# Moving half of a key gather from GpSimd to VectorE in a bilevel routing attention kernel

## What is computed

```python
xq = _quantize_active(x, BITA); wq = _quantize_weight(W, BITW)
x = conv(xq, wq) + b
q_reg = qr.mean(2); k_reg = kr.mean(2)
_, idx = jax.lax.top_k(einsum('brc,bsc->brs', q_reg, k_reg), 4)
kg = take_along_axis(kr[:, None], idx_e, axis=2)      # keys of 4 regions, 256 in all
vg = take_along_axis(vr[:, None], idx_e, axis=2)      # values of the same regions
attn = softmax(einsum('brqhd,brkhd->brhqk', qh, kh) * scale)   # 8 heads of 8
out = einsum('brhqk,brkhd->brqhd', attn, vh)
x = x + out @ wo + bo
x = x + gelu(layernorm(x) @ w1 + bm1) @ w2 + bm2
```

## Time and profile before

| | |
|---|---|
| median of 3 runs | 5986.81 us (5982.99 to 5993.53) |
| the profiled execution | 5993.37 us, its span 5991.5 us |
| mean granted TensorE clock | 0.861 of full speed |
| busy: TensorE, VectorE, ScalarE, GpSimd | 82%, 61%, 55%, 46% |
| steps | 1568 (16 pairs of 98) |
| first scores, last scores | 247.0 us, 5949.0 us |

### The profile page before, as it was taken

How to read it: one execution, slowest core, us unless ns; L and a number is a source line. 1 busy time by engine, 2 the same in 40 slices (tenths; PEclk the granted TensorE clock), 3 DMA queues, 4 the chain that set the end, 5 groups by cost and what they waited for, 6 DMA issues and landing times.

```text
span 5991.5 us, 184263 instructions
## 1 busy us (share of the span) xinstructions
PE 4903.3 (82%) x43666; PEld 3154.2 (53%) x43666; DVE 3655.8 (61%) x8855; ACT 3301.0 (55%) x6282; POOL 2770.8 (46%) x9656
## 2 busy tenths in 40 slices
PE   3388888888888888888888888888887888888888
PEld 1265555545555455555555555555554555555564
DVE  2266665656656565665666666565665766656565
ACT  1156555565555655555565555655555565555646
POOL 1345444454544545444454544545444454544543
PEclk8588988989888898888888889798888989888869
DMA  2433332323323333342333323333332333323311
GB/s 64 99 91 79 88 102 61 99 73 97 88 70 106 75 88 78 86 104 60 98 74 96 90 75 100 76 88 79 86 101 64 99 73 99 88 70 102 77 24 32
DMA packets 626976, 494.17 MB, mean 82 GB/s; under 512 B 483792, under 2 KB 613968, under 8 KB 615536
## 3 DMA queue, kind: packets, MB, share of 16 engines
q10 hardware_dynamic: 335360, 212.04, 15.6%
q1 hardware_dynamic: 290416, 268.94, 15.5%
HBM read 268.80 MB, written 211.94 MB: 80 GB/s over the span
## 4 chain that ended last, share of the span: by engine, by line
PE 40%; POOL 14%; POOLq 14%; issue 14%; DMA 7%; DVE 4%; ACT 3%; DVEq 2%; ACTq 1%; SPq 1%
PE ps L984 10%; POOLq L223 9%; POOL vg L490 7%; PE ps L998 7%; PE ps L1014 6%; POOL kg L475 4%; PE ps L877 3%; DMA max_d<-tr 3%; POOLq L224 2%; POOL xin L502 2%; PE ps L897 2%; DMA qm<-qk_d 2%; DVEq L223 2%; PE ps L970 2%; PE ps L893 2%
## 5 line engine op out<-in xcount | busy, mean ns | idle before, releaser
L717 DVE TENSOR_REDUCE mx<-ps 128x4 f32<-128x1024 f32 x1568 | 1921.7, 1226 | 1763.7 <-PE ps L984 1550.6
L828 ACT ACTIVATE pt<-ps 128x512 f32<-128x512 f32 x3136 | 1695.8, 592 | 1228.5 <-PE ps L998 1145.7
L490 POOL COPY vg<-vs 64x72 f32 x6272 | 1544.2, 246 | 1396.6 <-POOL kg L475 1064.6
L984 PE MATMUL ps<-kg,qm 96*128 96x256 f32 x6272 | 1381.2, 348 | 642.5 <-POOL kg L475 224.0
L984 PEld LDWEIGHTS ps<-kg,qm 96*128 96x128 f32 x6272 | 996.3, 214 | 1437.1 <-issue 1191.2
L475 POOL CAST kg<-ks 96x128 fp32r x3136 | 858.3, 298 | 1560.5 <-POOL vg L490 926.9
L998 PE MATMUL ps<-qm,kg 97*128 97x256 f32 x6272 | 1160.0, 310 | 110.9 <-DMA qm<-max_d 56.2
L1014 PE MATMUL ps<-pt,vg 128*32 128x128 f32 x25088 | 1139.1, 304 | 38.2 <-DVE um L707 22.6
L998 PEld LDWEIGHTS ps<-qm,kg 97*128 97x128 f32 x6272 | 985.6, 215 | 156.8 <-ACT pt L828 92.5
L1014 PEld LDWEIGHTS ps<-pt,vg 128*32 128x32 f32 x25088 | 653.8, 118 | 293.1 <-issue 72.2
L626 DVE CAST kg<-ks 96x128 fp32r x3136 | 622.5, 240 | 131.7 <-issue 124.3
(11 more groups left out here) (113 smaller groups left out, 4083.8 us busy)
## 6 DMA issues: line engine op xcount, KB each, us to landing
qk_d<-stg SPq DMA_DIRECT2D x224, 448.0 KB, 3.6
qm<-qk_d ACTq DMA_DIRECT2D x1792, 42.0 KB
ks<-qk_d ACTq DMA_DIRECT2D x96, 784.0 KB, 6.2
vs<-v_d ACTq DMA_DIRECT2D x64, 882.0 KB, 7.1
xin<-in_x SPq DMA_DIRECT2D x119, 224.0 KB, 2.6
xi_d<-xi SPq DMA_DIRECT2D x112, 224.0 KB, 2.3
qk_d<-stg SPq DMA_DIRECT2D x112, 224.0 KB, 3.0
max_d<-tr SPq DMA_DIRECT2D x1568, 2.0 KB
```

The costliest lines, as they stand in the source:

```text
L490: j = pool.tensor_copy(vg[slot][rows, (k // 2) * VW:(k // 2 + 1) * VW], vs[place(m)[0]][rows, bass.ds(region, 1), :].rearrange("p o n -> p ...
L717: v.tensor_reduce(mx[h % 2][:].rearrange("p (g j e) -> p g j e", g=2, j=2)[:, :, :, 0], ps[:, 0:2, :].rearrange("p g (j k) -> p g j k", j= ...
L828: act.activation(pt[m % 2][:, c], ps[:, 2 + c, :], ACT.Exp, scale=float(HD) ** -0.5).then_inc(S["pt_ready"], 1)
L984: i = pe.matmul(ps[:, g, 256 * j:256 * j + 256], qm[c % 2][0:NP3, t, g, 2 * j:2 * j + 2, :].rearrange("p h t -> p (h t)"), kg[slot][0:NP3, ...
```

## The change

GpSimd no longer gathers keys. VectorE copies the keys of all four regions; it loads four region numbers in place of two. GpSimd gathers the values alone, and the waits for its own earlier gathers are gone with the keys, as is the semaphore kp_ready. The values wait for the buffer of seven steps ago (u_full) and, at the first step of an image, for its loads.

```diff
-            for name in ("kd_ready", "kp_ready", "vg_ready"):
+            for name in ("kd_ready", "vg_ready"):
                 eng.wait_ge(S[name], p * STEPS + m)
...
-            def keys(p, m, kind):
-
-                slot = m % RING
-                if live(m - RING, kind) and not (kind == "last" and m >= STEPS):
-                    pool.wait_ge(S["st_full"], (p * STEPS + m - RING + 1) * 2)
-                    settled(pool)
-                if m >= AHEAD:
-                    pool.wait_ge(S["vg_ready"], p * STEPS + m - AHEAD)
-                    settled(pool)
-                gather_ready(pool, p, m)
-                for k, region in enumerate(regions(pool, regs, m, 2, 2)):
-                    j = pool.tensor_copy(kg[slot][0:NP3, :, 2 + k, :],
-                                         ks[place(m)[0]][0:NP3, :, bass.ds(region, 1), :].rearrange("p g o t -> p g (o t)"))
-                j.then_inc(S["kp_ready"], 1)
...
             def values(p, m, kind):
...
                     pool.wait_ge(S["u_full"], p * STEPS + m - RING + 1)
                     settled(pool)
-                ahead = m + AHEAD + 1
-                pool.wait_ge(S["kp_ready"], p * STEPS + (min(ahead, STEPS) if kind == "last" else ahead))
-                settled(pool)
+                gather_ready(pool, p, m)
...
-                if live(h + AHEAD, kind):
-                    keys(p, h + AHEAD, kind)
                 if live(h, kind):
                     values(p, h, kind)
...
-                for k, region in enumerate(regions(v, regs, m, 0, 2)):
+                for k, region in enumerate(regions(v, regs, m, 0, TOPK)):
                     j = v.tensor_copy(kg[slot][0:NP3, :, k, :],
...
                 pe.wait_ge(S["kd_ready"], T + 1)
-                pe.wait_ge(S["kp_ready"], T + 1)
```

More of the change, by code:

```diff
@@ L170, in build @@
             reg_full reg_ready logit_full lg_ready top_ready topi_ready
-            kd_ready kp_ready vg_ready sm_full mx_ready tr_ready st_full pt_ready u_full u_ready um_ready
+            kd_ready vg_ready sm_full mx_ready tr_ready st_full pt_ready u_full u_ready um_ready
             sum_full lns_ready rcs_ready un_ready y_full x2_ready xc2_full sq2_ready var2_full lnv2_ready rs2_ready
@@ L541, in before @@
                 pool.wait_ge(S["xq_done"], 1 + 2 * NW)
-                for m in range(AHEAD):
-                    keys(0, m, "lead")
             steps(pool, step, before)
```

## The result

The changed kernel takes 5693.43 us (median of 4 runs, 5666.08 to 5700.18) against 5990.17 us of the kernel before (median of 4 runs): a ratio of 0.950, 95% interval 0.948 to 0.952. In a second set of 5 runs, with fresh runs of the kernel before, the ratio was 0.9455 (0.9440 to 0.9469). The two intervals of this one kernel don't meet, so a difference of 0.005 between kernels of different sets is no more than sets differ by themselves. The profiled span is 5687.9 us where it was 5991.5.

A forecast was written before the change was run, and what follows sets the result against it. GpSimd's serial round of 3.2 us was taken to bound many steps from about 46, the ring of scores and maxima others. Terms: 81 + 115 + 30 - 60 + 30 = 196 us saved, giving 5790 us, range 5640 to 5940.

The forecast's parts named there:

- everything comes back: Rival, 14%: all 375 us of loop waits, 30 of last pair, 60 of clock return, 60 lost: 405 us, 5580.
- term 2: Other waits for GpSimd, mainly steps 60 to 98: 76 to 151 us come back, 115 taken.
- GpSimd's new round: GpSimd's value gathers: at most 1.82 us a round, below the fastest step of 2.12, so costed at nothing.
- Term 1: Steps 46 to 59 of the 15 pairs in the loop: 5.4 us a pair gained, 81 us.
- term 5: Clock in the loop, from step 60 on: shorter waits lift it, 30 us gained, bounds 0 and 105.
- Term 3: Last pair, 35 steps: 3.14 down to 2.27 us each with the clock up, 30 us gained.
- Term 4: VectorE's two more key copies a step put off the transposition by 0.3 us: 60 us lost, 120 at most.
- The wait moves on: Rival, 20%: in steps from 60 on other waits take over; only 71 us gained, 5916 us.
- Slower: Rival, 10%: VectorE's copies delay nearly each step by 0.3 us, 470 us lost against 256 won, 6200 us.

The follow-up runs named there:

- the kernel with twelve pieces: Changed kernel with GpSimd's value copies cut into twelve pieces, each step's behind the end of the last step's: 5698.7 us, ratio 0.9488.

## Why the prediction held, and where its sizes were off

The likeliest case came true: GpSimd's round left the path, and the time is inside the range. The mechanism was right and the sum too small: the gain was 297 us where the sum gave 196, half way to the 405 of "everything comes back". What is missing lies in two terms, the clock (some 70) and VectorE's copies (some 39); term 2 took 17 of it back. The total is inside the range because the range is wide, and the range was drawn a little short of what was said of it: it was to hold the bounds of all terms, and their far end is 5620, not 5640. Term by term:

- **GpSimd's new round at nothing: right**, and generous. Even a round of 2.83 us costs nothing in the loop.
- **Term 1, steps 46 to 59: 81 forecast, 83 measured.** The comparison of stretches with the same work was a sound price.
- **Terms 2 and 5, the other waits and the clock: 115 + 30 forecast, 197 measured in steps 60 to 98.** Term 2 was about right, and term 5 was the one that was mis-sized. TensorE's idle time ahead of the scores there falls by 12.0 us a pair (17.3 to 5.3), its other idle time rises by 5.5, so 6.5 come back: 0.54 of the wait, 98 us in 15 pairs, within the bounds of term 2 and a little under the 115 that I took. The other 6.6 us a pair are busy time. Time at the lower clock level falls by 13.7 us, and at half the speed that is up to 6.9 us of work: some 100 us for term 5, near its upper bound of 105, where I took 30. That this is the clock is worked out from the two traces; no run changed the clock alone in the changed kernel. The run with the scores twice shows only that the mean clock rose when TensorE was given more to do (0.861 to 0.937), and that the low level cost nothing while GpSimd set the pace.
- **Term 3, the last pair: 30 forecast, 36 measured** in its steps 26 to 60 (109.3 to 73.4), and 40 in the whole pair. The clock stayed up as said; the steps take 2.16 us (73.4 / 34), not 2.27, because the copies cost nothing there.
- **Term 4, VectorE's copies: 60 lost forecast, some 21 at most measured** in steps 0 to 46, where GpSimd had not bound, and those are not clear of the scatter. The step that failed is the reading of the earlier trace rows. I took a step with L707 and no idle time in brackets for one with nothing to spare. But the starts and durations there leave 0.09 us between transposition and `um` and 0.12 us between `um` and the maxima (5712.30 to 5712.39, 5712.69 to 5712.81), and the maxima began when the scores let them, 0.03 us behind their end. In the changed kernel the same ring of 2.12 us holds 0.27 us more of copies: the gaps are down to 0 and 0.05 us, and `um` takes 0.26 us for 0.30. The load of four numbers is also 184 ns shorter than that of two, which gives the longer register work its room.
- **The weighed rule.** The Trainium skill, Advanced Engine Details and Errata, Mode Summary, says that GpSimd and two-port Vector instructions block each other. I had not raised the term for it, and the copies didn't get slower. The page of the profile, before and after (busy us, mean ns of one):

```profile
L626 DVE CAST kg<-ks 96x128 fp32r x3136 | 622.5, 240 | 131.7 <-issue 124.3
L605 DVE CAST kg<-ks 96x128 fp32r x6272 | 1034.4, 226 | 99.2 <-issue 97.9
```

The traces say more than these means. Of VectorE's key copies in the kernel before, 41% ran beside no instruction of GpSimd: they take 216 ns on the mean, and none more than 250. Of those with more than 20 ns of GpSimd's work beside them 36% take more than 250 ns, and their mean is 258. In the changed kernel it is 217 ns for the ones alone, again none over 250, and 248 for the others, which are fewer (31% for 56%). So the trace agrees that VectorE's copies are held up when GpSimd works beside them, by 31 to 42 ns on the mean. That the port is the reason is the rule's word; no run isolates it.

- **The rivals.** "The wait moves on" is true of its places (L949, the way through DRAM) and false in size. "Everything comes back" had the clock at 60, nearer than my 30 and still short; of the waits in steps 60 to 98 about half came back, and not all. "Slower" did not come, but the kernel with the transposition first shows that its mechanism is real, at 0.56 us a step.

The sum of the terms as measured is 83 + 197 + 40 - 21 = 299.

## What to carry to other kernels

An engine at 46% can be the bound when its queue work stands in series with its data work: compare its whole round with the step, not its busy share. Where the results are buffered a few steps ahead, compare it with the mean step, less what else the engine does, and ask for a margin: 300 us of work in a pair of 342 cost nothing here, 337 in a pair of 360 did (that the margin made the difference is argued, see above). Only stretches longer than the lead feel the shortest step. And once a wait stands in an in-order queue, ask which address loads stand behind it: a small operation moved forward, with its wait, cost 870 us here; moved half as far, behind the first two copies, it cost nothing and seems to have gained a little.

## What the runs showed of the hardware that was not expected

- A register load of region numbers on VectorE takes 343 ns for four numbers, 527 for two and 747 for three. All of these start at a multiple of four numbers, so the start does not explain it.
- A key copy on VectorE takes 216 ns on the mean when GpSimd does nothing beside it, and 258 when it does (kernel before; 217 and 248 in the changed kernel). Beside the small copies of the kernel with twelve pieces it takes 228.
- Four more matmuls of 256 columns in each of 1568 steps cost 46 us against the runs beside them, 29 ns a step, where at the upper clock level they take some 0.5 us. The mean clock rose from 0.861 to 0.937 with them. Part of the rest is this kernel's and not the clock's: the first 46 steps of a pair paid 8.4 us, and GpSimd's longer lead gave 3.6 of them back in the next 14.
